# A float32 edge softmax: taking the maxima off in PSUM, in halves of 1024 columns, with part of the products on ScalarE

## The chip, the cores and the metric

One core of one Trainium2 chip. The metric is the device time of one launch in microseconds; less is better. The kernel is one program of four graph layers that run one after the other; the change touches the first of them only.

## The reference, cut to what matters

The first layer is an attention layer over E = 200,000 edges sorted by destination, with 16 x 16 = 256 logits per edge and a softmax of each of the 256 over the edges of one destination:

```
w_m = (efeat @ W_msg + b_msg).reshape(E, 16, -1)
w_a = (efeat @ W_attn + b_attn).reshape(E, 16, -1)
h_src = feat[src][:, :, None]
e1 = w_m * h_src
e2 = w_a * h_src
seg_max = segment_max(e2, dst)
ex = exp(e2 - seg_max[dst])
denom = segment_sum(ex, dst)
ft = segment_sum(e1 * (ex / denom[dst]), dst)
out = ft.sum(axis=1)
```

Its result goes through a layer normalisation into three more layers (a relational convolution, an edge-conditioned one and three convolutions with batch normalisation), which stay as they are. All is float32.

## The kernel before, in words

The edges are padded to 200,704 and cut into 128 chunks of T = 1568, one chunk to a partition. A block `b` takes TB0 = 8 neighbouring edges of every chunk (`q` = 0 to 7), so there are NB0 = 196 blocks; a tile `[128, 8, 256]` holds one block's 256 values per edge. The loop of blocks is written four at a time (U0 = 4), with four buffers of the loaded data, of the maxima M and of the sums ST, and two of e2, PX and cf.

Every engine has its own order of instructions, written out by hand, and they meet at semaphores only. `count(per, more)` in a wait is: so many per block in all blocks before, and `more` in this one.

- SP (`l0_sync`, L482) loads indices and turned edge features two blocks ahead, flags one block ahead, and stores the maxima and both kinds of sums, 1 MB each per block.
- POOL (`l0_pool`) gathers the eight source rows h of every partition, one indirect transfer for each q.
- TensorE (`weigh`, L543) multiplies the edge features of one q (17 rows, on one of four row groups of 32) with the attention or message weights, 256 float32 columns, into half a PSUM bank; one call does two q. Logits use banks 0 to 3, messages 4 to 7.
- VectorE (`l0_vector`) does the rest but the exponentials. For its block b: `logits` e2 = PSUM x h (L587), two q at a time; `forward` (L600) and `backward` (L608), the running maximum over the edges of one destination in both directions, a chain of 8 and one of 7 steps of 256 columns, each on the result of the last; `factor` (L620), the exponent cf that rescales the carried sums; and `less_maxima` (L614), e2 - M over all 2048 columns. For the block before, `last`: `exp_by_source` (L629), which multiplies the exponentials with h over 2048 columns; `carried` (L638); `messages` (L647), PSUM x that product, two q at a time; and `sum_step` (L654, L657), a chain of 8 running sums of 512 columns, numerator and denominator side by side.
- ScalarE (`l0_scalar`) takes Exp of cf (L571) and of all 2048 columns of e2 (L574).

The order of VectorE's instructions is that of `body` (L668). The steps of the three chains alternate there: between two steps of one chain stands an instruction of another.

Of the kernel before, what the change touches and what calls it, by code (L numbers as in the profile page):

```python
# [14 lines left out]
N, D = 6250, 16  # L15
# [105 lines left out]
def program(nc, io, out):  # L121
    ctx = ExitStack()
    with ctx:
# [337 lines left out]
        l_wa, l_wm, l_e2, l_fw, l_bw, l_a = sem("l_wa"), sem("l_wm"), sem("l_e2"), sem("l_fw"), sem("l_bw"), sem("l_a")  # L461
        l_ex, l_t, l_p, l_q, l_s = sem("l_ex"), sem("l_t"), sem("l_p"), sem("l_q"), sem("l_s")
# [4 lines left out]
        def l0_first_vector():  # L467
            V.memset(waug[:, :], 0.0).then_inc(*l_clear.up())
            V.memset(M[U0 - 1][:, TB0 - 1, :], 0.0).then_inc(*l_clear.up())
            V.memset(ST[U0 - 1][:, :, TB0 - 1, :], 0.0).then_inc(*l_clear.up())  # L470
            V.wait_ge(*l_clear.now())

# [9 lines left out]
        def l0_sync():  # L482
            def load_in(b):
                if due(n := b.on(-U0).count(4, 4)):
# [44 lines left out]
        def l0_pool():  # L529
            def gather(b):  # L530
                PO.wait_ge(l_in[b.k], b.slot(32, 32))
                if due(n := b.on(-U0).count(1, 1)):
                    PO.wait_ge(l_t, n)
                PO.nop(nofuse=True)
                for q in range(TB0):
                    PO.indirect_dma_start(h[b.k][:, q, :], None, io["x"],  # L536
# [5 lines left out]
        def l0_tensor():  # L542
            def weigh(b, n, message):  # L543
                if not message:
                    PE.wait_ge(l_in[b.k], b.slot(32, 32))
                if due(m := b.count(4, n - 1)):
                    PE.wait_ge(l_p if message else l_e2, m)
                for r in TWO:
                    row = 32 * (2 * (n % 2) + r)
                    mm = PE.matmul(PS[0:CH, 4 * message + 2 * (n % 2) + r, 0:C2], efT[b.k][row:row + D + 1, n // 2, :],  # L550
                                   waug[row:row + D + 1, C2 * message:C2 * message + C2])
                mm.then_inc(l_wm if message else l_wa, 1)

            def body(b):
                for n in range(4):
                    weigh(b, n, 0)
                if b.on(-1).exists():
                    for n in range(4):
                        weigh(b.on(-1), n, 1)

            def last(b):
                for n in range(4):
                    weigh(b, n, 1)
# [3 lines left out]
        def l0_scalar():  # L567
            def body(b):
                e, P = e2[b.k % 2], PX[b.k % 2]
                S.wait_ge(l_a, b.count(2, 2))  # L570
                S.activation(cf[b.k % 2][:, :], cf[b.k % 2][:, :], ACT.Exp).then_inc(l_ex, 1)  # L571
                if due(n := b.on(-2).count(TB0, TB0)):
                    S.wait_ge(l_s, n)
                S.activation(P[:, 0, :, :], e[:, :, :], ACT.Exp).then_inc(l_ex, 1)  # L574
# [3 lines left out]
        def l0_vector():  # L578
            def logits(b, n):
                ts = slice(2 * n, 2 * n + 2)  # L580
                if n == 0:
                    V.wait_ge(l_g[b.k], b.slot(16 * TB0, 16 * TB0))
                    if due(m := b.on(-2).count(2, 2)):
                        V.wait_ge(l_ex, m)
                V.wait_ge(l_wa, b.count(4, n + 1))
                bank = 2 * (n % 2)
                V.tensor_tensor(e2[b.k % 2][:, ts, :].rearrange("p t (i o) -> p t i o", i=D),  # L587
                                PS[0:CH, bank:bank + 2, 0:C2].rearrange("p t (i o) -> p t i o", i=D),
                                bc(h[b.k][:, ts, :], D, 3), ALU.mult).then_inc(l_e2, 1)

            def forward(b, q):
# [4 lines left out]
                V.wait_ge(l_e2, b.count(4, q // 2 + 1))  # L596
                if due(n := b.count(TB0, q)):
# [3 lines left out]
                                       in1=e2[b.k % 2][:, q, :], op0=ALU.add, op1=ALU.max).then_inc(l_fw, 1)  # L601
# [8 lines left out]

            def less_maxima(b):
                e = e2[b.k % 2]
                V.wait_ge(l_bw, b.count(TB0 - 1, TB0 - 1))
                V.tensor_tensor(e[:, :, :], e[:, :, :], M[b.k][:, :, :], ALU.subtract).then_inc(l_a, 1)  # L614
# [9 lines left out]
            def exp_by_source(b):  # L624
                P = PX[b.k % 2]
                V.wait_ge(l_ex, b.count(2, 2))
                if due(n := b.on(-2).count(TB0, TB0)):
                    V.wait_ge(l_s, n)
                V.tensor_tensor(P[:, 1, :, :].rearrange("p t (i o) -> p t i o", i=D),  # L629
                                P[:, 0, :, :].rearrange("p t (i o) -> p t i o", i=D),  # L630
                                bc(h[b.k][:, :, :], D, 3), ALU.mult).then_inc(l_t, 1)

            def carried(b):
                if due(n := b.slot(32, 0)):
                    V.wait_ge(l_st[b.k], n)
                if due(n := b.count(TB0, 0)):
# [4 lines left out]
            def messages(b, n):  # L641
                ts = slice(2 * n, 2 * n + 2)
                P = PX[b.k % 2]
                V.wait_ge(l_t, b.count(1, 1))
                V.wait_ge(l_wm, b.count(4, n + 1))
                bank = 4 + 2 * (n % 2)
                V.tensor_tensor(P[:, 1, ts, :], PS[0:CH, bank:bank + 2, 0:C2], P[:, 1, ts, :], ALU.mult).then_inc(l_p, 1)  # L647

            def sum_step(b, q):
                s, P = ST[b.k], PX[b.k % 2]  # L650
                V.wait_ge(l_p, b.count(4, q // 2 + 1))
                if q == 0:
                    V.wait_ge(l_q, b.count(1, 1))
                    V.tensor_tensor(s[:, :, 0, :], s[:, :, 0, :], P[:, :, 0, :], ALU.add).then_inc(l_s, 1)  # L654
                else:
                    V.wait_ge(l_s, b.count(TB0, q))
                    V.scalar_tensor_tensor(out=s[:, :, q, :], in0=s[:, :, q - 1, :], scalar=flb[b.k][:, q, 1:2],  # L657
                                           in1=P[:, :, q, :], op0=ALU.mult, op1=ALU.add).then_inc(l_s, 1)

            def sums_alone(b):  # L660
                exp_by_source(b)
                carried(b)
                for q in range(TB0):
                    if q % 2 == 0:
# [3 lines left out]
            def body(b):  # L668
                last = b.on(-1) if b.on(-1).exists() else None
                logits(b, 0)  # L670
                logits(b, 1)
# [1423 lines left out]
```

## Time and profile before

| | us |
|---|---|
| median of 3 runs | 14537.35 (14511.41 to 14591.29) |
| profiled execution | 14542.93 |
| its span, first to last instruction | 14541.7 |
| VectorE busy in the span | 11137.2 (77%) |
| TensorE busy | 8238.6 (57%) |
| ScalarE busy | 4787.7 (33%) |
| POOL busy | 8838.1 (61%) |

The first layer's blocks run from about 190 to 4480 us of the span. The page's second part cuts the span into 40 slices of 364 us; in the slices of the first layer VectorE shows 9 (90% or more), TensorE 2 and ScalarE 0 or 1, and the granted TensorE clock is 5 tenths of full speed; later layers show TensorE at 4 to 9 and the clock at 5 to 9 tenths. Busy time counts only how long instructions ran; how they follow one another is read from the timeline.

### The profile page before, as it was taken

How to read it: one execution, taken by the hardware profiler on the slowest of the kernel's cores; microseconds unless marked ns; L12 is line 12 of the kernel's file. 1: busy time of each engine (PE TensorE's matmuls, PEld its weight loads, DVE VectorE, ACT ScalarE, POOL GpSimd, SP SyncE). 2: the span in 40 equal slices, each digit the busy share in tenths (PEclk: the TensorE clock that was granted, in tenths of full speed). 3: DMA queues.
4: the chain of work that ended last, by engine and by line, in shares of the span. 5: the costliest groups of instructions: out<-in, count | busy, mean ns of one | idle time of the engine just before them, and what ended most of it. 6: DMA issues, size and time to landing. Idle time of an engine off the chain costs nothing. (4 is left out here: it accounts for less than half of the span.)

```text
span 14541.7 us, 147837 instructions
## 1 busy us (share of the span) xinstructions
PE 8238.6 (57%) x41291; PEld 5764.4 (40%) x41291; DVE 11137.2 (77%) x19230; ACT 4787.7 (33%) x2765; POOL 8838.1 (61%) x6976
## 2 busy tenths in 40 slices
PE   1222222222220489689746565665678858985886
PEld 0111111111110367567523233332456646664664
DVE  6999999999998768578645455554578868886886
ACT  0110110110110368467501110110057746774774
POOL 5555555555553377678745555555168857885886
PEclk5555555555555799899867787777789979997997
DMA  2444444444442222222211111111033323332332
GB/s 81 157 150 155 157 152 153 157 154 151 157 155 94 68 68 84 60 71 82 55 45 37 38 36 37 36 35 38 16 102 111 112 74 105 112 106 80 111 110 70
DMA packets 629773, 1371.10 MB, mean 94 GB/s; under 512 B 262833, under 2 KB 403118, under 8 KB 554126
## 3 DMA queue, kind: packets, MB, share of 16 engines
q1 hardware_dynamic: 405534, 1076.25, 20.2%
q0 software_dynamic: 224112, 293.30, 8.8%
q8 instruction: 62, 1.02, 0.0%
q14 instruction: 65, 0.53, 0.0%
HBM read 656.16 MB, written 712.80 MB: 94 GB/s over the span
## 5 line engine op out<-in xcount | busy, mean ns | idle before, releaser
L536 POOL DMA_INDIRECT h<-in_x,idx x1568 | 2252.1, 1436 | 2000.3 <-DMA efT<-in_edge_attr_t 1561.3
L550 PE MATMUL PS<-waug,efT 17*128 17x256 f32 x6272 | 1129.7, 679 | 3165.9 <-DVE e L587 2178.7
L1684 PE MATMUL PS<-hot,lhs 128*128 128x392 bf16 x9408 | 1829.2, 352 | 1221.8 <-issue 644.4
L1671 POOL DMA_INDIRECT myg<-node_table,mix x1568 | 1644.5, 1049 | 1310.0 <-DVE mmsg L1740 782.1
L550 PEld LDWEIGHTS PS<-waug,efT 17*128 17x128 f32 x6272 | 696.7, 314 | 3598.4 <-DVE e L587 2225.4
L1684 PEld LDWEIGHTS PS<-hot,lhs 128*128 128x128 bf16 x9408 | 949.9, 102 | 2101.4 <-issue 1028.9
L1305 PE MATMUL PS<-every_weight,dstf 112*128 112x144 f32 (+1 forms) x8960 | 1346.4, 296 | 533.2 <-DVE dstf L1405 376.1
L1305 PEld LDWEIGHTS PS<-every_weight,dstf 112*128 112x128 f32 x8960 | 1268.1, 200 | 717.6 <-DVE dstf L1405 197.1
L1755 DVE TENSOR_TENSOR lhs<-mkx,m 128x512 bf16<-128x512 bf16 x1176 | 428.9, 419 | 1402.8 <-remote 1065.4
L571 ACT ACTIVATE cf<-cf 128x256 f32<-128x256 f32 x196 | 81.7, 417 | 3842.8 <-DVE e L614 3842.8
L1283 POOL DMA_INDIRECT c0yg<-node_table,c0ix x672 | 935.8, 1393 | 533.1 <-DMA c0ix<-in_src 287.4
L1283 POOL DMA_INDIRECT c2yg<-node_table,c2ix x672 | 952.9, 1418 | 276.6 <-issue 204.5
L1283 POOL DMA_INDIRECT c1yg<-node_table,c1ix x672 | 944.9, 1406 | 289.5 <-issue 204.2
L657 DVE SCALAR_TENSOR_TENSOR ST<-ST,flb,PX 128x512 f32<-128x512 f32 x1372 | 1016.3, 741 | 0.7
L1283 POOL DMA_INDIRECT r1yr<-node_table,r1ix x672 | 832.0, 1238 | 283.0 <-issue 204.2
L1283 POOL DMA_INDIRECT r0yr<-node_table,r0ix x672 | 828.4, 1233 | 271.0 <-issue 204.2
L1335 ACT ACTIVATE r0hot<-r0hb 128x3584 fp32r<-128x3584 bf16 x224 | 717.0, 3201 | 535.5 <-DVE r0hb L1391 329.9
L1295 PE MATMUL PS<-c2hot,parts 128*112 128x512 f32 x3136 | 842.7, 416 | 34.7 <-ACT c2hot L1335 29.2
L1295 PE MATMUL PS<-c0hot,parts 128*112 128x512 f32 x3136 | 840.8, 415 | 32.3 <-ACT c0hot L1335 27.1
L1295 PE MATMUL PS<-c1hot,parts 128*112 128x512 f32 x3136 | 834.7, 413 | 33.4 <-ACT c1hot L1335 27.6
L1335 ACT ACTIVATE r1hot<-r1hb 128x3584 fp32r<-128x3584 bf16 x224 | 716.9, 3201 | 396.4 <-DVE r1hb L1391 196.8
L1295 PE MATMUL PS<-r1hot,parts 128*112 128x512 f32 x3136 | 811.6, 410 | 25.4 <-ACT r1hot L1335 25.0
(393 smaller groups left out, 18688.7 us busy)
## 6 DMA issues: line engine op xcount, KB each, us to landing
softmax_maxima<-M SPq DMA_DIRECT2D x196, 1024.0 KB, 8.2
softmax_denominators<-ST SPq DMA_DIRECT2D x196, 1024.0 KB
softmax_numerators<-ST SPq DMA_DIRECT2D x196, 1024.0 KB
r0rb<-pick_b SPq DMA_DIRECT2D x56, 512.0 KB
r0ra<-pick_a SPq DMA_DIRECT2D x56, 512.0 KB
r1rb<-pick_b SPq DMA_DIRECT2D x56, 512.0 KB
r1ra<-pick_a SPq DMA_DIRECT2D x56, 512.0 KB
c0rb<-pick_b SPq DMA_DIRECT2D x56, 512.0 KB
```

What stands on the lines that cost most here:

```text
L536: PO.indirect_dma_start(h[b.k][:, q, :], None, io["x"], bass.IndirectOffsetOnAxis(ap=idx[b.k][:, q:q + 1], axis=0))\
L550: mm = PE.matmul(PS[0:CH, 4 * message + 2 * (n % 2) + r, 0:C2], efT[b.k][row:row + D + 1, n // 2, :], waug[row:row + D + 1, C2 * message:C ...
L571: S.activation(cf[b.k % 2][:, :], cf[b.k % 2][:, :], ACT.Exp).then_inc(l_ex, 1)
L657: V.scalar_tensor_tensor(out=s[:, :, q, :], in0=s[:, :, q - 1, :], scalar=flb[b.k][:, q, 1:2], in1=P[:, :, q, :], op0=ALU.mult, op1=ALU.ad ...
L1283: PO.indirect_dma_start(to, None, table, bass.IndirectOffsetOnAxis(ap=ix[b.k][:, q:q + 1], axis=0))\
L1295: mm = PE.matmul(PS[0:A9 * D, 4 + q % 2, :], parts[:, m % 2, m // 2, :], hot_[q % 2][:, m // 2, :], start=(m == 0), stop=(m == 2 * KT - 1))
L1305: mm = PE.matmul(weighed(q)[:, r, 0:R * D], mx[q % 2][:, 128 * r:128 * r + 128], every[0:A9 * D, 0:R, :].rearrange("p r o -> p (r o)"))
L1335: S.activation(hot_[q % 2][:, :, :], hb[q // 2 % 2][:, :, at:at + 512], ACT.Copy).then_inc(h_cv.sem, 1)
L1671: PO.indirect_dma_start(yg[b.k][:, q, :], None, table8, bass.IndirectOffsetOnAxis(ap=ix[b.k][:, q:q + 1], axis=0))\
L1684: mm = PE.matmul(PS[:, 6 + k, 0:A7 // 2], lhs[(G * b.k + q) % 2][:, r, part, :], hot[4 * ((G * b.k + q) % 2) + r][:, k * A7 // 2:(k + 1) * ...
L1755: V.tensor_tensor(lhs[(G * b.k + q) % 2][:, :, n, :].rearrange("p t (a f) -> p t a f", a=8), mkx[b.k][:, 4 * q:4 * q + 4, :, :], bc(m3[b.k ...
```

## The change

- The eight q of a block are laid out by `at(q) = 2 * (q % 4) + q // 4`: bank n holds q = n and q = n + 4. A bank is now full (512 columns), all four logit banks `wa` belong to one block until its exponentials are taken, and likewise the four message banks `wm`.
- Weights, logits and messages work on halves: half 1 is banks 2 and 3 (q 2, 6, 3, 7), half 0 banks 0 and 1. A half is four matmuls of 256 columns and one VectorE instruction of 1024 columns. The logits' weights of half 1 wait for the Exp of half 1 of the block before, those of half 0 for its Exp of half 0.
- `less_maxima` leaves VectorE. TensorE first copies the logits e2 back into their bank by a matmul with the identity (`put_back`, 128 rows, 512 float32 columns, an open accumulation), and when the backward steps that a bank needs are done it adds minus identity times M (`less_maxima`). The order is bank 3, 2, 1, 0; bank 3 needs four backward steps, bank 0 all seven.
- ScalarE takes Exp straight from PSUM, half 1 first, then Exp of cf, then makes the product with h for tiles 6 and 7 (q 3 and 7) by 32 ACTIVATE instructions of 16 columns each, with h as the per-partition scale. `exp_by_source` keeps the other six tiles (1536 columns). The messages of half 1 wait for ScalarE's products.
- The order of VectorE is new; backward 0 to 6 stand together, and so do sum steps 4 to 7.

```diff
+        minus = sb("minus_ident", [128, 128], F32, L)
+        wa = PS[0:CH, 0:4, :].rearrange("p b (t c) -> p (b t) c", c=C2)
+        wm = PS[0:CH, 4:8, :].rearrange("p b (t c) -> p (b t) c", c=C2)
+        def at(q):
+            return 2 * (q % 4) + q // 4
         def l0_first_vector():
+            V.tensor_scalar(minus[:, :], ident[:, :], -1.0, None, ALU.mult).then_inc(*vd.up())
...
         def l0_tensor():
+            def weigh(b, half, message):
+                if message:
+                    if due(m := b.on(-1).count(2, half + 1)):
+                        PE.wait_ge(l_p, m)
+                else:
                     PE.wait_ge(l_in[b.k], b.slot(32, 32))
+                    if due(m := b.on(-1).count(3, 2 - half)):
+                        PE.wait_ge(l_ex, m)
+                for q in (2 * half, 2 * half + 1, 2 * half + 4, 2 * half + 5):
+                    row = 32 * (q % 4)
+                    mm = PE.matmul((wm if message else wa)[:, at(q), :], efT[b.k][row:row + D + 1, q // 4, :],
                                    waug[row:row + D + 1, C2 * message:C2 * message + C2])
                 mm.then_inc(l_wm if message else l_wa, 1)
+            def put_back(b, n):
+                PE.wait_ge(l_e2, b.count(2, 2 - n // 2))
+                PE.matmul(PS[0:CH, n, :], ident[:, :], e2[b.k % 2][:, 2 * n:2 * n + 2, :], start=True, stop=False)
+            def less_maxima(b, n):
+                PE.wait_ge(l_bw, b.count(TB0 - 1, TB0 - 1 - n))
+                mm = PE.matmul(PS[0:CH, n, :], minus[:, :], M[b.k][:, n::4, :], start=False, stop=True)
+                if n % 2 == 0:
+                    mm.then_inc(l_le, 1)
             def body(b):
+                for half in (1, 0):
+                    weigh(b, half, 0)
                 if b.on(-1).exists():
+                    for half in TWO:
+                        weigh(b.on(-1), half, 1)
+                for n in (3, 2, 1, 0):
+                    put_back(b, n)
+                for n in (3, 2, 1, 0):
+                    less_maxima(b, n)
...
         def l0_scalar():
+            def exp_half(b, half):
+                S.wait_ge(l_le, b.count(2, 2 - half))
                 if due(n := b.on(-2).count(TB0, TB0)):
                     S.wait_ge(l_s, n)
+                S.activation(PX[b.k % 2][:, 0, 4 * half:4 * half + 4, :], wa[:, 4 * half:4 * half + 4, :], ACT.Exp).then_inc(l_ex, 1)
+            def body(b):
+                exp_half(b, 1)
+                exp_half(b, 0)
+                S.wait_ge(l_a, b.count(1, 1))
+                S.activation(cf[b.k % 2][:, :], cf[b.k % 2][:, :], ACT.Exp).then_inc(l_ex, 1)
+                S.wait_ge(l_ex, b.count(3, 2))
+                for t in (6, 7):
+                    for i in range(D):
+                        act = S.activation(PX[b.k % 2][:, 1, t, D * i:D * i + D], PX[b.k % 2][:, 0, t, D * i:D * i + D], ACT.Copy,
+                                           scale=h[b.k][:, t, i:i + 1])
+                act.then_inc(l_x, 1)
...
-                V.tensor_tensor(e[:, :, :], e[:, :, :], M[b.k][:, :, :], ALU.subtract).then_inc(l_a, 1)
...
+                V.tensor_tensor(P[:, 1, 0:6, :].rearrange("p t (i o) -> p t i o", i=D),
+                                P[:, 0, 0:6, :].rearrange("p t (i o) -> p t i o", i=D),
+                                bc(h[b.k][:, 0:6, :], D, 3), ALU.mult).then_inc(l_t, 1)
```

VectorE's `body` after the change, in order (calls with `last` are left out in the first block):

```
logits(b, 1)   logits(b, 0)   forward(b, 0)   exp_by_source(last)   forward(b, 1)   carried(last)
forward(b, 2)  messages(last, 0)  forward(b, 3)  forward(b, 4)  sum_step(last, 0)  forward(b, 5)
forward(b, 6)  sum_step(last, 1)  forward(b, 7)  messages(last, 1)  backward(b, 0) ... backward(b, 6)
sum_step(last, 2)  sum_step(last, 3)  factor(b)  sum_step(last, 4) ... sum_step(last, 7)
```

POOL's gather waits also for `l_x` of four blocks ago, and the input load for both message halves of four blocks ago.

## Rows read from the trace of the kernel before

**Rows 1.** Windows: stretch, length, busy time of each engine, clock, DMA share, GB/s.
```profile
200.00:4400.00 4200.00, 1107.74 (x6163) 684.57 (x6165) 4132.09 (x6744) 427.59 (x386) 2231.40 (x1551) 0.50 0.42 153
```
**Rows 2.** Groups by form, 400 to 4200 us: count, busy, mean ns, idle before.
```profile
L647 DVE TENSOR_TENSOR PX<-PS,PX 128x512 f32<-128x512 f32 x698 | 474.4, 680 | 0.0
...
L614 DVE TENSOR_TENSOR e<-e,M 128x2048 f32<-128x2048 f32 x175 | 398.9, 2279 | 0.0
L574 ACT ACTIVATE PX<-e 128x2048 f32<-128x2048 f32 x174 | 329.5, 1894 | 0.0
```
**Rows 3.** Waits, 400 to 4200 us: who waited for whom, total, times, longest.
```profile
ACT cf L571 <- DVE e L614: 3404.6, 174, 19.6
...
DVE e L587 <- PE PS L550: 58.2, 174, 0.3
```
**Rows 4.** Timeline, VectorE, one block: start, duration, instruction.
```profile
1999.47 2.27 DVE L614 TENSOR_TENSOR e<-e,M 128x2048 f32<-128x2048 f32 x1
...
2019.79 0.48 DVE L608 SCALAR_TENSOR_TENSOR M<-M,flb 128x256 f32<-128x256 f32 x1
2020.19 0.74 DVE L657 SCALAR_TENSOR_TENSOR ST<-ST,flb,PX 128x512 f32<-128x512 f32 x1
2020.85 0.47 DVE L620 SCALAR_TENSOR_TENSOR cf<-M,flb 128x256 f32<-128x256 f32 x1
...
2021.25 2.28 DVE L614 TENSOR_TENSOR e<-e,M 128x2048 f32<-128x2048 f32 x1
2023.45 0.74 DVE L657 SCALAR_TENSOR_TENSOR ST<-ST,flb,PX 128x512 f32<-128x512 f32 x1
```
**Rows 5.** Timeline, VectorE, the first block.
```profile
205.32 3.48 DVE L600 SCALAR_TENSOR_TENSOR M<-M,flb,e 128x256 f32<-128x256 f32 x6
...
208.84 4.04 DVE L608 SCALAR_TENSOR_TENSOR M<-M,flb 128x256 f32<-128x256 f32 x7
```
**Rows 6.** Timeline, the last block's sums.
```profile
4469.43 1.22 PE L550 MATMUL PS<-waug,efT 17*128 17x256 f32 x4 [9.27 <-DVE PX L647]
...
4471.59 1.60 DVE L657 SCALAR_TENSOR_TENSOR ST<-ST,flb,PX 128x512 f32<-128x512 f32 x2
...
4473.11 0.68 DVE L647 TENSOR_TENSOR PX<-PS,PX 128x512 f32<-128x512 f32 x1
4473.83 1.60 DVE L657 SCALAR_TENSOR_TENSOR ST<-ST,flb,PX 128x512 f32<-128x512 f32 x2
```
**Rows 7.** Timeline, TensorE in a later layer: one record, eight, eight.
```profile
5039.84 0.58 PE L1305 MATMUL PS<-every_weight,dstf 112*128 112x128 f32 x1 [3.65 <-DVE dstf L1405]
...
5039.84 2.07 PE L1305 MATMUL PS<-every_weight,dstf 112*128 112x128 f32 x8 [3.65 <-DVE dstf L1405]
...
5046.65 1.06 PE L1305 MATMUL PS<-every_weight,dstf 112*128 112x128 f32 x8
```
**Rows 8.** Timeline and windows of two bursts after pauses, columns as in Rows 1.
```profile
10954.20 2.28 PE L1305 MATMUL PS<-every_weight,dstf 112*128 112x144 f32 x8 [4.44 <-DVE dstf L1405]
...
10954.20:10957.20 3.00, 3.00 (x11) 2.75 (x12) 3.00 (x7) 3.00 (x2) 2.70 (x2) 0.50 0.55 200
10957.20:10957.45 0.25, 0.25 (x2) 0.20 (x1) 0.25 (x2) 0.25 (x1) 0.25 (x1) 0.77 0.00 0
...
14296.00 2.29 PE L1305 MATMUL PS<-every_weight,dstf 112*128 112x144 f32 x8 [4.22 <-DVE dstf L1405]
...
14296.00:14302.00 6.00, 6.00 (x18) 4.89 (x19) 5.41 (x11) 6.00 (x4) 5.08 (x4) 0.50 0.39 126
14302.00:14302.50 0.50, 0.50 (x3) 0.38 (x2) 0.50 (x2) 0.50 (x1) 0.50 (x1) 0.62 0.90 361
```
**Rows 9.** ScalarE: a group by form, and two rows of the timeline.
```profile
L2008 ACT ACTIVATE mean<-mean 128x16 f32<-128x16 f32 x2 | 0.4, 216 | 193.2 <-DVE mean L1987 193.2
...
4487.62 0.31 ACT L762 ACTIVATE w<-w 128x128 f32<-128x128 f32 x1 [21.77 <-DVE w L795]
...
4487.84 0.29 ACT L763 ACTIVATE w<-w 128x128 f32<-128x128 f32 x1
```

More of the change, by code:

```diff
@@ L471, in l0_first_vector @@
             V.wait_ge(*l_clear.now())
+            V.wait_ge(*vd.now())
         def l0_first_sync():
@@ L561, in last @@
             def last(b):
-                for n in range(4):
-                    weigh(b, n, 1)
+                for half in TWO:
+                    weigh(b, half, 1)
             loop(PE, body, NB0, TB0, last=last, u=U0)
         def l0_scalar():
[L568 to L571, printed above, removed]
+            def exp_half(b, half):
+                S.wait_ge(l_le, b.count(2, 2 - half))
@@ L576, in l0_scalar, with logits @@
             loop(S, body, NB0, TB0, u=U0)
         def l0_vector():
-            def logits(b, n):
-                ts = slice(2 * n, 2 * n + 2)
-                if n == 0:
+            def logits(b, half):
+                ts = slice(4 * half, 4 * half + 4)
+                if half == 1:
                     V.wait_ge(l_g[b.k], b.slot(16 * TB0, 16 * TB0))
[L583 to L586, printed above, removed]
+                V.wait_ge(l_wa, b.count(2, 2 - half))
@@ L587, in logits @@
                 V.tensor_tensor(e2[b.k % 2][:, ts, :].rearrange("p t (i o) -> p t i o", i=D),
-                                PS[0:CH, bank:bank + 2, 0:C2].rearrange("p t (i o) -> p t i o", i=D),
+                                wa[:, ts, :].rearrange("p t (i o) -> p t i o", i=D),
                                 bc(h[b.k][:, ts, :], D, 3), ALU.mult).then_inc(l_e2, 1)
@@ L669, in body @@
                 last = b.on(-1) if b.on(-1).exists() else None
+                logits(b, 1)
                 logits(b, 0)
-                logits(b, 1)
                 forward(b, 0)
-                logits(b, 2)
+                if last:
+                    exp_by_source(last)
                 forward(b, 1)
-                logits(b, 3)
+                if last:
+                    carried(last)
                 forward(b, 2)
                 if last:
-                    exp_by_source(last)
+                    messages(last, 0)
                 forward(b, 3)
-                if last:
-                    carried(last)
                 forward(b, 4)
                 if last:
-                    messages(last, 0)
+                    sum_step(last, 0)
                 forward(b, 5)
+                forward(b, 6)
+                if last:
+                    sum_step(last, 1)
+                forward(b, 7)
                 if last:
                     messages(last, 1)
-                forward(b, 6)
-                if last:
-                    sum_step(last, 0)
-                forward(b, 7)
-                if last:
-                    sum_step(last, 1)
-                backward(b, 0)
+                for n in range(7):
+                    backward(b, n)
                 if last:
                     sum_step(last, 2)
-                backward(b, 1)
-                if last:
-                    messages(last, 2)
-                backward(b, 2)
-                if last:
-                    sum_step(last, 3)
-                backward(b, 3)
-                if last:
-                    sum_step(last, 4)
-                backward(b, 4)
-                if last:
-                    messages(last, 3)
-                backward(b, 5)
-                if last:
-                    sum_step(last, 5)
-                backward(b, 6)
-                if last:
-                    sum_step(last, 6)
+                    sum_step(last, 3)
                 factor(b)
-                less_maxima(b)
-                if last:
-                    sum_step(last, 7)
+                for q in range(4, TB0):
+                    if last:
+                        sum_step(last, q)
             loop(V, body, NB0, TB0, last=sums_alone, u=U0)
```

52 lines of the change are left out of this document (20 added, 32 removed).

## The prediction, made before the changed kernel was run

> **What bounds the kernel now.** The windows come first: in the stretch of the first layer VectorE is busy 4132 of 4200 us, TensorE 1108 at a granted clock of 0.50, ScalarE 428 [rows 1]. The groups of that stretch and the waits say the same: ScalarE's idle time is a wait for the subtraction L614, and VectorE itself waits only for the logits' weights, 0.33 us a block (58.2 us over 174) [rows 2, 3]. So a block lasts as long as VectorE's instructions follow one another. The timeline gives their spacing: L614 begins at 1999.47 and again at 2021.25, so a block is 21.78 us, and there are 196. There also an instruction that does not need the one in front starts 0.08 us before that one's end: a step follows a 256-column one after 0.40 (duration 0.48), a sum step after 0.66 (0.74), L614 after 2.20 (2.28) [rows 4].
>
> **What leaves VectorE's block.** L614 goes: 2.20. L629 falls from 2048 to 1536 columns; between 512 columns (0.680) and 2048 (2.279) a column costs 1.04 ns, so 0.53 [rows 2]. Four logit and four message instructions of 512 columns become two and two of 1024: 4 x 0.60 against 2 x (0.680 + 0.534 - 0.08) = 2.27, so 0.13 for each kind, 0.26. The 0.33 wait was for a matmul that started only after the first logits; the new weights of a half are asked for before them, and I take it as gone (what is late in its place comes below). Sum: 3.32.
>
> **What the new order adds.** Before, between two steps of one chain stood an instruction of another chain. The new order puts dependent steps back to back: forward 3-4 and 5-6, all of backward 0 to 6, sum steps 2-3 and 4-5-6-7. Counting the pairs: 2 + 6 + 4 = 12, and forward 0 right behind the second logits. The first block, which has no sums of a predecessor, shows what such a pair costs: six forward steps take 3.52 us from 205.32 to 208.84, 0.587 each, not 0.40; so +0.19 [rows 5]. In the last block two sum steps take 1.60 together, so they start 0.86 apart, not 0.66: +0.20; and a sum step starts 0.72 behind the message instruction that it needs, not 0.60: +0.12 [rows 6]. Sum: 8 x 0.19 + 4 x 0.20 + 0.12 = 2.44. VectorE's own block becomes 21.78 - 3.32 + 2.44 = 20.90, 0.88 less.
>
> The Trainium skill, "VectorE: DVE Perf Modes", section "The DRAIN you can't avoid", speaks against that addition: instructions with and without a semaphore between them took the same time. By it the 2.44 is nothing and VectorE's block 18.46 us. This trace does not agree for this chain (0.587 against 0.40 for one line of one kernel); the rival that follows from it is below.
>
> **The new path through TensorE and ScalarE.** The maxima are now taken off in PSUM. Let t = 0 be when the matmul for bank 3 may begin, just behind the fourth backward step. VectorE then has two steps at 0.587, one at 0.40, sum 2 0.86, sum 3 0.66, factor 0.40, sums 4 to 6 at 0.86 and sum 7 0.66: the next block's first logits (half 1) could start at 6.78 and the second (half 0) at 7.91. Before them lie, in this order: four matmuls of `minus` by 512 float32 columns; weights of half 1 (their banks are free after the first Exp, which fits beside the last two matmuls); Exp of half 0; weights of half 0; logits.
> - A matmul: eight records of 128 float32 columns take 2.07 us at the low clock (1.2 GHz) and 1.06 at the high one (2.4 GHz) [rows 7]. There are two records to a float32 matmul; one alone lasts 0.58, so they follow at (2.07 - 0.58) / 7 = 0.213 us per 128 columns; 512 columns in two records are 1.70 us low and 0.85 high. Four: 6.82 or 3.41.
> - Exp of 1024 columns: between 16 columns (0.216, [rows 9]) and 2048 (1.894, [rows 2]) a column is 0.826 ns: 1.05.
> - Weights of a half: two matmuls on two row groups took 1.22 at the low clock [rows 6], 0.85 of it columns. The half has four on two row groups, so 2.07 low, and about 1.1 high (bounds 0.7, if all four ran side by side, and 2.07).
> - So the second logits may start at e + 0.30 (drain) + 0.06 + 1.05 + 0.06 + 1.1 + 0.05 = e + 2.6, where e is when the four matmuls have streamed. They are late when e > 5.3. The first logits (e + 1.15 against 6.78) are never the tighter ones.
>
> e hangs on the clock. It is 0.50 through the whole stage now [rows 1]. After a pause of over 4 us a dense burst starts at the low clock and gets the high one later: in 38 such bursts of this trace after 3.1 to 6.4 us, mean 4.5; the shortest and the longest are shown (0.50 for 3.00 us, then 0.77 in the next 0.25; 0.50 for 6.00, then 0.62 in the next 0.50) [rows 8]. The new TensorE stream has that form. Behind the four matmuls come the weights and the four copies of e2 back into PSUM, done near t = 13, and the next four matmuls start at 20.9: a pause of about 8 us, and each burst starts low. If the clock rises at r, e = 3.41 + r/2, late for r > 3.78; over the 38 values of r the mean lateness is 0.5 us a block. It lies on VectorE's path, since nothing is queued there ahead of the logits. The ends for this wait are 0 and 2.50 (all low: 6.82 + 0.30 + 0.06 + 1.05 + 0.06 + 2.07 + 0.05 = 10.41 against 7.91). I take 0.5.
>
> **ScalarE's 32 products.** They begin near t = 7.4 (e 5.67, both Exps, `cf` 0.41) and must be done for the messages of half 1, 9.5 us behind the second logits, at 17.9: 10.5 us for 32, or 0.33 each. The nearest rows: a 16-column ACTIVATE lasts 0.216, and a 128-column one follows its predecessor by 0.22 [rows 9]; so 4.4 (0.216 less an overlap of 0.08) to 7.0 us. Hidden, price 0; without the cover each 0.1 us more per product than 0.33 would be 3.2 us a block. The Trainium skill, "ScalarE: Activation LUTs", section "What ACT_TABLE_LOAD costs", adds a fixed piece of about 93 ns for a per-partition scale, and an overlap of the same size; an estimate by it is 32 x 0.20 = 6.4 us, hidden too; no row before has such a scale.
>
> **Nothing.** The four copies back start at t = 9 and even at the low clock end before 17, ahead of 20.9. Input loads wait on SP for the message weights and gathers on POOL additionally for ScalarE's products of four blocks ago; both are prefetched two blocks and long met. The maxima are stored earlier, the sums as before. DMA is at 0.42 [rows 1] and would be at 0.43. `minus` is one instruction of under 0.3 us.
>
> **Sum.** -0.88 + 0.5 = -0.38 us a block, x 196 = -74 us. The profiled execution took 14543 (span 14541.7); so 14469, and the median of the runs, 14537, lies 6 below the profiled one. I say 14468, with 14410 to 14525 for this case (lateness 0.2 to 0.8).
>
> **Rivals.**
> - *TensorE is never late* (the clock stays high over the pause, or rises at once): -0.88 a block, -172 us, 14370. For it: pauses of 4.1 to 4.3 us sometimes left the clock high. Against: none of more than 5 us did, and this one is 8. Chance 0.13.
> - *The matmuls run at the low clock and TensorE sets the block* (slower). Place: between the fourth backward step and the second logits. All low: -0.88 + 2.50 = +1.62, +318 us, 14861. It decides from a mean lateness of 0.88, that is from e = 6.2 or from weights that need 0.4 us more than my 1.1. For it: the stage is at 0.50 now and my margin is thin. Against: float32 bursts later in this trace do get the high clock [rows 8]. Chance 0.24, most of it between +0 and +150.
> - *ScalarE's products are late*: above 0.33 us each; at 0.40 the block is 2.2 us longer and the time 14900. Chance 0.05.
> - *Back-to-back chains cost nothing*: block 18.46; but then the 6.78 and 7.91 shrink by 1.4, lateness is about 1.6, and the block 20.1: -1.7, -335 us, 14208. Only a change of behaviour between first block and loop would bring it. Chance 0.03. The section on the drain named above is its ground.
> - My forecast: 0.55.
>
> **How the numbers follow.** About 0.5% (73 us) is what a measurement can tell here. The forecast lies on that bound, so half of its 0.55 is faster by more and half is not. Faster: 0.26 of it, with the first rival's 0.13 and the fourth's 0.03, is 0.42. Same: 0.27 of it and 0.05 of the second rival, 0.32. Slower: the second rival's other 0.19, ScalarE's 0.05, and 0.02 of my own case: 0.26. The range runs from 14360 (first rival) to 14650 (the second up to a lateness of 1.45); outside are the drain rival, ScalarE's and the upper third of the second, under 0.2.
>
> **What would show it.** In the profile after: no L614 group on VectorE, L629's at about 1.75 us; backward steps 0.58 to 0.59 apart; float32 matmuls of 128x512 at two durations, the subtraction mostly in the slow one and the copies back in the fast one; granted clock of the stage between 0.55 and 0.8; the only VectorE wait in the stage before the half-0 logits, on TensorE, 0.2 to 0.8 us a block; ScalarE idle before its next Exp. Wrong if the clock stays 0.50, if VectorE waits for the products, or if the wait is above 0.9 us.

## The result: slower, by a stall that no step of the prediction had

The changed kernel took 14751.52 us (median of 4 runs, 14720.96 to 14781.33) against 14534.86 (14511.41 to 14591.29) for the kernel before on the same chip: ratio 1.0143, 95% interval 1.0107 to 1.0180, so 1.4% slower. I had said 14468, faster, 14360 to 14650. The profiled execution took 14740.64, its span 14739.4.

The windows of the first layer after the change, columns as in [rows 1], do not look like a slower kernel: VectorE is less busy than before, TensorE more, at a higher clock.

```profile
200.00:4400.00 4200.00, 2467.52 (x8742) 1154.34 (x8743) 3577.29 (x5452) 1581.45 (x6361) 1572.93 (x1465) 0.74 0.40 145
```

VectorE's busy time fell from 4132 to 3577 us of 4200, and it is still the engine that sets the stage. The rest is idle time, and the waits (400 to 4200 us, columns as in [rows 3]) name it:

```profile
DVE e L625 <- issue: 331.1, 58, 8.3
DVE e L625 <- PE PS L567: 61.3, 66, 1.4
DVE M L638 <- DVE e L625: 34.3, 165, 0.2
DVE ST L692 <- DVE ST L692: 19.5, 41, 0.5
```

"issue" is a wait for nothing that the profile shows. The timeline of VectorE (start, duration, instruction, idle time before it) shows it in front of the first logits of every fourth block; rows in between are left out:

```profile
1907.09 2.41 DVE L625 TENSOR_TENSOR e<-PS,h 128x1024 f32<-128x1024 f32 x2
...
1927.87 2.52 DVE L625 TENSOR_TENSOR e<-PS,h 128x1024 f32<-128x1024 f32 x2 [0.20 <-PE PS L567]
...
1939.81 3.61 DVE L646 SCALAR_TENSOR_TENSOR M<-M,flb 128x256 f32<-128x256 f32 x7
1943.34 1.60 DVE L692 SCALAR_TENSOR_TENSOR ST<-ST,flb,PX 128x512 f32<-128x512 f32 x2
...
1945.26 3.31 DVE L692 SCALAR_TENSOR_TENSOR ST<-ST,flb,PX 128x512 f32<-128x512 f32 x4
1956.47 2.36 DVE L625 TENSOR_TENSOR e<-PS,h 128x1024 f32<-128x1024 f32 x2 [7.90 <-issue]
1959.05 0.48 DVE L638 SCALAR_TENSOR_TENSOR M<-M,flb,e 128x256 f32<-128x256 f32 x1 [0.22 <-DVE e L625]
...
1978.13 2.41 DVE L625 TENSOR_TENSOR e<-PS,h 128x1024 f32<-128x1024 f32 x2 [1.39 <-PE PS L567]
...
1996.63 2.48 DVE L692 SCALAR_TENSOR_TENSOR ST<-ST,flb,PX 128x512 f32<-128x512 f32 x3 [0.47 <-DVE ST L692]
1999.23 2.41 DVE L625 TENSOR_TENSOR e<-PS,h 128x1024 f32<-128x1024 f32 x2
```

The blocks take 20.8, 28.6, 21.7 and 21.1 us, and so on: 92.1 for four. Four blocks are one pass of the loop, so the 7.9 us (8.3 at the most) lie at its back edge, the jump from its last instruction to its first, and 1.4 more follow one block later. The mean of 40 passes is 92.16. TensorE explains neither the place nor the length. It works at its own weights in the first 2.1 us of the gap, then waits for VectorE; only afterwards is it slow and late:

```profile
1941.92 5.53 PE L577 MATMUL PS<-M,minus_ident 128*128 128x512 f32 x8 [8.30 <-DVE M L646]
1947.37 3.30 PE L567 MATMUL PS<-waug,efT 17*128 17x256 f32 x32
1957.75 6.14 PE L573 MATMUL PS<-e,ident 128*128 128x512 f32 x8 [7.08 <-DVE e L625]
1970.37 6.66 PE L577 MATMUL PS<-M,minus_ident 128*128 128x512 f32 x8 [6.48 <-DVE M L646]
```

The page's third part has another trace of it (queue, kind: packets, MB, share). One of the two lines of instruction queues was `q14 instruction: 65, 0.53, 0.0%` before and is now:

```profile
q14 instruction: 299, 2.44, 0.0%
```

The other line, `q8 instruction`, hardly moved (62 and 64 packets). A packet of q14 is 8 KB (2.44 MB over 299). Asked for in short windows, the new packets come five to a pass; in the pass above they start at 1945.41, 1948.91, 1954.74, 1958.63 and 1997.32, two of them inside the gap (1948.57 to 1956.47) and the last 0.7 us behind the end of the 0.47 wait. The reading that the experiments put to the test: VectorE's instructions are fetched anew in each pass, and it waits for them.

From the first logits to the first copy out of PSUM behind the layer the stage was 4284.1 us and is 4525.1: +241.0. The whole profiled execution is only 197.7 longer; the later layers, which the change does not touch, took about 44 less, and I have no cause for that.

### The profile page after: what moved, and what is told of

It reads as the page before. It is cut to its first block and busy times, and to the rows that moved or that the text cites. A ratio compares the mean times of both kernels' runs of the same rounds, so it can differ in the third digit from the quotient of the medians.

```text
span 14739.4 us, 160571 instructions
## 1 busy us (share of the span) xinstructions
PE 9775.6 (66%) x44427; PEld 6319.8 (43%) x44427; DVE 10793.1 (73%) x18251; ACT 6059.7 (41%) x9233; POOL 8359.8 (57%) x6976
## 3 DMA queue, kind: packets, MB, share of 16 engines
q14 instruction: 299, 2.44, 0.0%
## 5 line engine op out<-in xcount | busy, mean ns | idle before, releaser
L549 POOL DMA_INDIRECT h<-in_x,idx x1568 | 1683.1, 1073 | 2810.4 <-DMA efT<-in_edge_attr_t 1858.4
L1689 POOL DMA_INDIRECT myg<-node_table,mix x1568 | 1682.3, 1073 | 1275.3 <-DVE mmsg L1758 750.0
L577 PE MATMUL PS<-M,minus_ident 128*128 128x512 f32 x1568 | 1167.1, 913 | 1495.3 <-DVE M L646 1488.6
L603 ACT ACTIVATE PX<-PS 128x1024 f32<-128x1024 f32 x392 | 401.3, 1024 | 2809.8 <-PE PS L577 2251.8
L577 PEld LDWEIGHTS PS<-M,minus_ident 128*128 128x128 f32 x1568 | 452.8, 304 | 2201.2 <-DVE M L646 1749.5
L613 ACT ACTIVATE PX<-PX,h 128x16 f32<-128x16 f32 x6272 | 1264.3, 295 | 8.8 <-issue 8.8
L573 PE MATMUL PS<-e,ident 128*128 128x512 f32 x1568 | 866.4, 703 | 353.2 <-DVE e L625 342.3
```

The source lines that it names most:

```text
L549: PO.indirect_dma_start(h[b.k][:, at(q), :], None, io["x"], bass.IndirectOffsetOnAxis(ap=idx[b.k][:, q:q + 1], axis=0))\
L573: PE.matmul(PS[0:CH, n, :], ident[:, :], e2[b.k % 2][:, 2 * n:2 * n + 2, :], start=True, stop=False)
L577: mm = PE.matmul(PS[0:CH, n, :], minus[:, :], M[b.k][:, n::4, :], start=False, stop=True)
L613: act = S.activation(PX[b.k % 2][:, 1, t, D * i:D * i + D], PX[b.k % 2][:, 0, t, D * i:D * i + D], ACT.Copy, scale=h[b.k][:, t, i:i + 1])
L1689: PO.indirect_dma_start(yg[b.k][:, q, :], None, table8, bass.IndirectOffsetOnAxis(ap=ix[b.k][:, q:q + 1], axis=0))\
```

## The experiments

A *filler* is a number of one-column memsets on VectorE ahead of the first layer's loop (0.06 us each, and 240 in a row take 7.1). They move the code; the first logits wait for their data meanwhile and start within 1 us of where they did:

```
         V.wait_ge(*vd.now())
+        filler = sb("filler", [128, N], F32, L)
+        for k in range(N):
+            V.memset(filler[:, k:k + 1], 0.0)
```

The places 209 to 429 and the like in the first expectations leave out the separate wait and register instructions. In the compiled stream the loop of the changed kernel is 269 instructions, 318 to 586, and that of the kernel before 303, 339 to 641; the table uses these. "Stage" is measured as above; it was 4284.1 us for the kernel before. The runs fall into four groups on different chips; the median of the kernel before, run beside each, was 13686 (e1 to e4), 13661 (one run, e5 to e8), 13700 (e9 to e12) and 14493 us (e13 to e15). The first layer takes the same on all of them (4284.1, 4283.8 and 4284.2 for two-page forms of the kernel before; 4525.1 and 4525.9 for the changed one), so whole times are compared only within a group, stages everywhere. After, e1, e9, e12, e13 and e15 are medians of 4 or 5 runs, the others are single runs, and the effects read from them are read from the stage.

| run | loop at (start mod 256) | pages touched | q14 packets | stage | whole |
|---|---|---|---|---|---|
| after, as given | 318 (62) | 3 | 299 | 4525.1 | 14751.52 |
| e13, the same again | 318 (62) | 3 | 298 | 4525.9 | 14716.28 |
| e5, filler 256 | 574 (62) | 3 | 300 | 4508.4 | 13924.48 |
| e14, filler 249 | 567 (55) | 3 | 300 | 4369.9 | 14575.66 |
| e9, filler 4 | 322 (66) | 2 | 68 | 4036.6 | 13454.85 |
| e1, filler 32 | 350 (94) | 2 | 69 | 4034.8 | 13443.15 |
| e2, filler 64 | 382 (126) | 2 | 70 | 4036.3 | 13457.96 |
| e10, filler 240 | 558 (46) | 2 | 70 | 4036.6 | 13445.77 |
| e3, before, filler 32 | 370 (114) | 2 | 66 | 4283.8 | 13701.49 |
| e6, before, filler 239 | 577 (65) | 2 | 67 | 4284.2 | 13678.14 |
| e11, before, filler 215 | 553 (41) | 3 | 296 | 4290.4 | 13719.44 |

"Pages" are taken here as runs of 256 instructions whose boundaries lie at 64 modulo 256. The rows of the table leave 63 to 65; the idle times pick 64, since one falls in front of place 320 in the changed kernel and one between 575 and 578 in e14. What the rows do not fix is the length: runs of 128 with a boundary at 64 modulo 128 fit them as well, with four touched where the table says 3 and three where it says 2. The traces speak for the 128: each packet is 8 KB, the stream has just passed 448 and 576 at two of the five packets of a pass of the changed kernel, and the 0.47 wait is in front of place 448, in the middle of a page of 256. A loop of this length that starts at 180 to 191 modulo 256 would decide it; no run has one. "Page" and "three pages" below can be read either way.

**e1, filler 32.**


> The changed kernel with 32 one-column memsets of a spare tile on VectorE ahead of the first layer's loop, nothing else: its loop of 220 instructions then stands at instructions 241 to 461 of VectorE's program and not at 209 to 429. Theory (fetch of VectorE's loop): in the changed kernel VectorE idles 7.9 us at each back edge of the first layer's loop, where the loop before, at 226 to 472, idled nothing; the loop now lies across a boundary of the instruction memory, and every jump back waits for a fetch. With the shift the 7.9 us go; 47 iterations, so some 370 to 400 us less than the changed kernel, near 14350 to 14400, faster than before by about 1%. Rival (ScalarE's 32 small instructions a block, or TensorE's longer loop, are what is fetched and waited for): nothing changes, 14750.

Blocks of 20.48 us, no stall: 0.9821 of the kernel before (0.9805 to 0.9837). The stage is 490 us shorter and not 370 to 400, since the waits that follow the stall go with it. The lost time is the stall, and the place of the code decides on it.

**e2, filler 64, and e3, the kernel before with filler 32.**


> The same with 64 memsets: the loop stands at 273 to 493. Theory: boundaries are 256 instructions apart; both kernels' behaviour puts one 30 to 39 instructions short of a count of 256 and the next at 473 to 482, so this loop crosses the second one and the 7.9 us at each jump are back: within 40 us of the changed kernel's 14750. Rival (the filler helps because it delays the start or separates the engines): like the run with 32.

> The kernel before with the same 32 memsets: its loop of 246 instructions moves from 226-472 to 258-504. Theory: it then crosses the second boundary and gets a stall of about 8 us at each of its 47 jumps, +350 to +400 us, 14900, with nothing of the change in it. Rival (the stall comes from the new work on ScalarE and TensorE): 14537, no change.

Both missed: no stall, 20.48 and 21.78 us a block. The distance of the loop's ends to a boundary, as I counted it then, is not the rule.

**e4, products on VectorE.** ScalarE's `for t in (6, 7)` products and their waits go, VectorE's product has `0:8` for `0:6`; the loop starts at the same place and has 268 instructions.


> The changed kernel with ScalarE's 32 products a block left to VectorE again (one instruction of 2048 columns for all eight tiles), and the waits for them gone; ScalarE's loop falls from 163 to 31 instructions, VectorE's stays at 209 to 429. Theory: the 7.9 us at each jump stay; each block costs 0.53 us more on VectorE, 104 us in all, if none of it is hidden: 14800 to 14860. Rival (ScalarE's instruction stream causes the stall): it goes, 14750 - 380 + 104 = 14470.

The stall stayed (7.9 to 8.3 us, 295 packets, stage 4562.8), with ScalarE's loop some 130 instructions shorter. So it is not ScalarE's stream; that it is VectorE's, e1 had shown, whose fillers stand in VectorE's stream alone.

**e5, filler 256, and e6, the kernel before with filler 239.**


> 256 one-column fills ahead of VectorE's loop of the first layer instead of 32: the loop lies at its instructions 465 to 685, that is 256 further than in the changed kernel (209 to 429), which stalled 7.9 us at each back edge; with 32 fills (241 to 461) and 64 (273 to 493) there was no stall. Theory A (the place within 256-instruction pages decides; the Trainium skill, Runtime: NRT & Kernel Launch, section Instruction fetch mechanics, states such pages): the stall is back, blocks of 20.8 to 21.1 us and one of 29 in every four, the stage about 4525 us, the instruction queue near 300 packets. Theory B (another period, or the absolute place): no stall, blocks of 20.48, the stage near 4036 us, some 70 packets.

> The kernel before with 239 one-column fills: its VectorE loop lies at 465 to 711 instead of 226 to 472. Nothing of the change is in it. Theory A (a loop that begins some instructions ahead of a page of 256 and reaches far into the next one loses its first page, whatever it computes): a stall of about 8 us each four blocks, the stage 4284 + 46 x 8.5 = 4675 us, the whole about 390 us above the kernel before. Theory B (the stall needs the new order or the new path through TensorE): the stage stays at 4284 us and the time at that of the kernel before plus some 20 us for the fills.

e5 brings the stall back, as a period of 256 (or of 128) wants. e6 missed: no stall, stage 4284.2. That sent me to the compiled stream, and to pages *touched* by the loop.

**e9, filler 4, and e10, filler 240**: on either side of the twelve starts (52 to 63) from which 269 instructions touch three pages.


> Only 4 one-column fills ahead of VectorE's loop. Counted with the separate wait instructions, the compiled loop of the changed kernel is 269 instructions long (318 to 586; the counts in the expectations so far left the waits out), that of the kernel before 303 (339 to 641). The places so far agree with pages of 256 instructions of which two are held, with a boundary at 64 modulo 256: the changed kernel (start 62) and the one with 256 fills (start 574, which is 62) touch three pages, the first with two instructions; the kernel before with 239 fills (start 577, which is 65) touches two and did not stall. Theory A (three pages): with 4 fills the start is 66, two pages, no stall: blocks of 20.48, stage near 4036 us, time near 0.982 of the kernel before. Theory B (the end near a boundary, within the first third of a page, makes the stall): the end moves only from 74 to 78, the stall stays, stage 4508 to 4525 us.

> 240 fills: the loop lies at 558 to 826, modulo 256 from 46 to 58. Theory A (a third page is needed only if the loop starts at 52 to 63): two pages, no stall, stage near 4036 us. Theory B (the loop starts ahead of a boundary and ends in the first third of a page behind another): the stall is there, stage 4508 to 4525 us.

Theory A held in both: no stall, stages of 4036.6. Four instructions worth nothing are worth 489 us of stage (4525.9 in e13 against 4036.6). e9's waits, 400 to 4000 us, in full:

```profile
DVE M L641 <- DVE e L628: 36.6, 176, 0.2
DVE e L628 <- PE PS L570: 3.1, 20, 0.2
```

and its row of the instruction queue:

```profile
q14 instruction: 68, 0.56, 0.0%
```

**e11, the kernel before with filler 215.**


> The kernel before with 215 fills: its loop of 303 instructions lies at 553 to 855, modulo 256 from 41. Its pages are three (boundary at 64: 23 instructions, 256, 24). Theory A: it stalls now, about 8 us each four blocks (46 back edges, 370 us): stage near 4650 us where the same kernel with 239 fills had 4284, time near 14050. Rival (only the changed kernel's code stalls): 4284 us, 13680.

Half right. The kernel before makes the fetches now, 296 packets for the 67 of e6, with its code as it was:

```profile
q14 instruction: 296, 2.42, 0.1%
```

But it loses 0.12 to 0.2 us a pass and not 8. VectorE's sequencer, which takes instructions from the stream and runs some way ahead of the engine, shows where a part of the rest is. Its rows (`DVEq`) of the loop's line have the jump back and the first instruction behind it; duration in ns, then the start. e11, and e9 for comparison:

```profile
L100 DVEq COMPARE_BRANCH  x1: 63/63/63, 2023.9 to 2023.9; - x1
L100 DVEq FUSED_REGOPS  x1: 63/63/63, 2026.7 to 2026.7; - x1
```
```profile
L100 DVEq COMPARE_BRANCH  x1: 56/56/56, 2084.3 to 2084.3; - x1
L100 DVEq FUSED_REGOPS  x1: 63/63/63, 2084.6 to 2084.6; - x1
```

The step over the jump takes 0.3 us with two pages and, with three, 2.8 in e11, 2.9 in the changed kernel and 3.0 in e14. So e11 has this stall too and hides it: when its sequencer jumps at 2023.9, VectorE still has the subtraction (2024.02, 2.27 us) and a sum step in hand, until 2026.96, and the next logits start at 2026.99. The changed kernel has only one sum step in hand there, until 0.7 us behind the jump. The second half of the 7.9 is missing in e11: the next packet comes 2.4 us after the one at the jump, in the changed kernel and in e14 5.8 us after it. e11's first page holds 23 instructions (at 87.1 us for 303 some 6.6 us of work) and its third 24, where the changed kernel has 2 and 11. That this split makes the difference is argued and not shown.

**e13, the changed kernel again.**


> The changed kernel itself, unchanged, beside the others of this call: its loop touches three pages. Expected: a stall of 7.9 us each four blocks, stage 4508 to 4525 us, and some 480 us more than with 4 fills (13455 when it ran), so 13930, a ratio to the kernel before of 1.015 to 1.02. If it ran near 13460 here, the stall would hang on something else than the place of the code.

1.0152 (1.0114 to 1.0190), the stall as before.

**e14, filler 249**: the same loop, 9 instructions in the first page and 4 in the third.


> 249 fills: VectorE's loop lies at 567 to 835, modulo 256 from 55: 9 instructions in the first page (two of registers, both logits, forward 0 and their waits), 256, and 4 in a third. Theory: three pages make two fetches one after the other at each back edge, and what stalls is the second, which comes 7.9 us after VectorE has run dry in the changed kernel; the instructions in the first page cover a part of it. Both logits and forward 0 take 2.8 us, so the idle time is 5.1 us, in front of the source-row product and no longer of the logits. Stage 4036 + 47 x (5.1 + 0 to 1.4 follow-up) = 4280 to 4345 us. Rival (the stall is one length whatever lies in the first page): 7.9 us, 4508 or more. Rival (it belongs to logits alone): none.

VectorE's waits, 400 to 4000 us, and the two of one pass:

```profile
DVE PX L665 <- issue: 106.3, 40, 2.9
DVE e L628 <- issue: 103.4, 41, 2.8
DVE e L628 <- PE PS L570: 50.2, 88, 1.2
```
```profile
1984.09 2.36 DVE L628 TENSOR_TENSOR e<-PS,h 128x1024 f32<-128x1024 f32 x2 [2.52 <-issue]
...
1989.66 1.76 DVE L665 TENSOR_TENSOR PX<-PX,h 128x1536 f32<-128x1536 f32 x1 [2.51 <-issue]
```

The sum, 5.0, is the 5.1 I had worked out (7.9 less 2.8 of work in the first page), but it comes in two pieces: 2.5 at the back edge, and 2.5 where the second page begins (place 576 in this stream, the source-row product). In both kernels the stream goes on behind that boundary 8.5 to 8.6 us after the jump. In the changed kernel nothing of VectorE's data work lies in the first page, its boundary is in front of the logits, and one gap of 7.9 is all that is seen. The stage is above my 4280 to 4345: a pass takes 88.75 us, 6.8 more than in e9, of which the two pieces are 5.2 on average and the waits for TensorE 1.2. The rest is not accounted for.

**e7, subtraction on VectorE, and e8, products on VectorE**, both with filler 32. e7 puts `tensor_tensor(e, e, M, subtract)` back behind the factor, drops `put_back` and `less_maxima` from TensorE and lets Exp read `e2`; e8 is e4's edit.


> The changed kernel with 32 fills (no stall) and the maxima taken off by VectorE again, one instruction of 2048 columns behind the factor; no float32 matmuls with identity or its negative, Exp reads SBUF. If the PSUM path is worth what my sum gave it (2.20 a block and nothing late): 20.48 + 2.20 = 22.7 us a block, the stage 4036 + 431 = 4467 us. Rival: the matmuls cost VectorE time that the order hid, then the block is shorter than 22.5.

> The changed kernel with 32 fills (no stall) and all source-row products on VectorE: its instruction has 2048 columns for 1536, ScalarE has no products. By my sum 0.53 us a block more: 21.0 us, the stage 4036 + 104 = 4140 us. Rival: the 32 instructions of ScalarE slow VectorE (they share SBUF) or delay it; then the block is shorter than 20.9.

Per block, from the stages 4446.1, 4201.5 and e1's 4034.8 over 196: the subtraction in PSUM is worth 2.10 us (my term: 2.20), the products on ScalarE 0.85 (0.53). Of the latter 0.3 is a wait of VectorE for TensorE's weights that came up in e8 (53.8 us over 86 in 400 to 4000). So e7 came near its 4467, and e8 missed its 4140. Each rests on one run. In e7, without the float32 matmuls of 512 columns, the granted clock of the stage is back at 0.50 (0.83 in e9).

**e12 and e15, other orders of VectorE's work**, both with filler 4. (l logits, f forward, b backward, s sum, m messages, x source product, c carried, F factor.)

```
after: l1 l0 f0 x f1 c f2 m0 f3 f4 s0 f5 f6 s1 f7 m1 b0..b6 s2 s3 F s4..s7
e12:   l1 l0 x f0 c f1 m0 f2 s0 f3 m1 f4 s1 f5 f6 f7 b0..b4 s2 b5 s3 b6 s4 F s5..s7
e15:   l1 l0 x f0 c f1 m0 f2 s0 f3 m1 f4 f5 f6 f7 b0..b4 s1 b5 s2 b6 s3 F s4..s7
```


> 4 fills and another order of the same VectorE instructions: source-row product directly behind the second logits, messages of half 1 between forward 3 and 4, sum 1 between forward 4 and 5, sums 2, 3 and 4 between backward 4, 5, 6 and the factor. One dependent pair of maxima steps (0.12) and two of sum steps (0.20) less, and no wait of 0.20 for forward 0: 0.7 us a block, 19.8, stage 3900 us, 135 us below filler 4 alone. Between the fourth backward step and the second logits VectorE has 7.3 us of work, and TensorE and ScalarE needed about 7.4. Rival: TensorE's path is now the later one; VectorE waits 0.5 us or more before the half-0 logits, and the block stays at 20.3 or above.

> The interleaved order had VectorE waiting 0.69 us a block for the half-1 weights: from the first matmul of the burst to the first logits 6.67 us, and VectorE's work in that stretch is 6.0. Here sum 1 also moves behind backward 4 (sums 1, 2, 3 between backward 4, 5, 6 and the factor, sums 4 to 7 behind it): one sum step of 0.66 more in the stretch, 6.8 in all, so nothing is late. Against filler 4: three dependent pairs of sums for four (0.20) and no wait at forward 0 (0.20): 0.4 us a block, 20.08, stage 3955 us, 80 us less than 13455: 13375. Rival: the chain through TensorE and ScalarE is itself 20.48 long around the block whatever VectorE's order, then 4036 again.

e12 gained nothing over e9 (13451.45 and 13454.85): VectorE's order is 0.7 us a block shorter and it waits 0.7 for TensorE. The waits of e12 in 400 to 4000 us, and of e15:

```profile
DVE e L628 <- PE PS L570: 125.5, 176, 0.8
```
```profile
DVE e L628 <- PE PS L570: 50.0, 156, 0.5
DVE e L628 <- issue: 12.9, 50, 0.4
```

e15 missed too: blocks of 20.28 to 20.73 us where 20.08 was due, stage 4045.9, 0.9822 of the kernel before (0.9790 to 0.9854). The groups of the subtraction on TensorE in e9 and in e15 show what gave way, the mean time of one:

```profile
L580 PE MATMUL PS<-M,minus_ident 128*128 128x512 f32 x1408 | 955.4, 838 | 1442.3 <-DVE M L649 1442.3
```
```profile
L580 PE MATMUL PS<-M,minus_ident 128*128 128x512 f32 x1408 | 1048.7, 914 | 1348.7 <-DVE M L649 1348.7
```

A longer stretch behind the fourth backward step was eaten by a slower burst (914 ns for 838; 862 in e12); the granted clock of the stage fell from 0.83 to 0.80.

Two limits that happen to meet do not explain this. From the sixth pass on a pass takes 81.92 us on average, four times 20.48, in e1, e2, e9, e10, e12 and e15 alike, in three orders of VectorE's work (each pass within 0.03 us of it, in e15 within 0.25); in e9 it comes down to that from 84.24, in e1 up from 81.80. The windows of one block of e9 and one of e12, cut where the granted clock changes, columns as in [rows 1]:

```profile
2013.59:2020.41 6.82, 3.50 (x4) 1.50 (x5) 6.57 (x13) 0.00 (x0) 4.99 (x6) 0.50 0.05 5
2020.42:2034.07 13.65, 8.72 (x45) 4.30 (x43) 13.11 (x19) 8.69 (x35) 3.54 (x3) 1.00 0.65 244
```
```profile
2009.97:2016.79 6.82, 3.78 (x5) 1.72 (x6) 6.51 (x14) 0.00 (x0) 5.30 (x6) 0.50 0.05 5
2016.80:2030.44 13.64, 8.58 (x44) 4.20 (x43) 12.74 (x18) 8.69 (x35) 4.21 (x4) 1.00 0.65 244
```

The clock goes low and high once in each block, and rises 3.5 us behind the start of the burst of subtractions in e9 (2016.91), 3.8 us behind it in e12 (2013.01) and 4.1 to 4.9 in e15. A block that tries to be shorter has its burst start earlier against the rise, with more of its matmuls at the low clock, and so the time comes back as a wait for TensorE. That the block is held in step with the clock in this way is what the figures suggest; no run holds the clock and changes the order, so it is not shown.

## Why the prediction was wrong

**The step that failed is "Sum": -0.38 us a block, times 196.** It took all blocks as alike, and the paragraph "Nothing" had no entry for the way VectorE gets its instructions. Shorter by 34 instructions, the loop also began 21 earlier in the stream, at 62 for 83 modulo 256, and so touched three pages for two. Each pass of four blocks then costs 7.90 at the back edge, 0.47 in front of place 448, 1.39 for TensorE's lateness behind the stall, and 0.20 in front of one more pair of logits: 9.96 of the 92.08 - 4 x 20.48 = 10.16 that a pass takes more than four blocks of e9. Over 47 passes that is 478 us; e13 less e9 measures 489. With it, my own 14468 would have been near 14950, so the rest of the sum erred by some 200 us the other way: 21.40 us a block where e9 has 20.48, 180 us, and the later layers. That the measured time lies where the slower rival had its numbers (up to 14861) is luck: its place and its cause were others.

The Trainium skill, "Runtime: NRT & Kernel Launch", section "Instruction fetch mechanics", states blocks of 256 instructions, two of them held, sequential prefetch, and a fetch before execution goes on when a taken branch leaves the window. I did not weigh it. The runs agree with the stall at a taken branch (2.8 to 3.0 us for 0.3 at the jump) and with two blocks held, if a block is 256 instructions; by the 8 KB packets and the wait at place 448 what is fetched at a time may be 128. They show the price that the page does not give (7.9, 5.0 or 0.1 us a pass), and add that the loop of the kernel before is above 256 instructions as well and costs nothing so long as it touches two.

**The other steps, read from e9 where the stall is gone:**
- *What leaves the block, 3.32*: held as far as runs show it. e7 gives 2.10 for the subtraction (2.20), and the source-row product took 1.75 as said; the other 0.59 has no run of its own.
- *What the order adds, 2.44*: too much. Seven backward steps take 3.61, so (3.61 - 0.48) / 6 = 0.52 each in the loop and not the 0.587 of the first block [rows 5]: 8 x 0.07 = 0.5 less. Sum pairs held (1.60 for two, 0.85 apart). Forward 0 starts 0.21 behind the end of the second logits, 0.29 later than an independent instruction and not 0.12. My 20.90 becomes 20.54; measured 20.48.
- *Lateness, 0.5*: nothing (3.1 us in 3600). The matmuls of the subtraction lasted 0.84 us a record, the copies back 0.61, so the burst did start slow. The size that was wrong is r: I took 38 values of other bursts, mean 4.5, with lateness above 3.78, and in e9 it was 3.48 to 3.53 in every block from 20 to 180. With 3.5 my path gives 7.8 us from the start of the burst to the second logits; they start at 7.7 (its 0.30, 0.06 and 0.05 stand on no row). Where VectorE does wait for TensorE, 0.7 in e12 and 1.4 in the changed kernel, it is in front of the first logits, which I had called never the tighter ones.
- *ScalarE's products*: hidden. All 32 took 6.44 us, 0.20 each, the estimate of 6.4; a single one lasts 0.295, longer than my nearest row:

```profile
L613 ACT ACTIVATE PX<-PX,h 128x16 f32<-128x16 f32 x5280 | 1063.2, 295 | 0.0
```
- *The rivals*: the slower one named TensorE at the low clock; the place was wrong, and the stage's clock rose from 0.50 to 0.74. "TensorE is never late" (14370) is what e9 shows once the stall is gone: -1.30 us a block with the cheaper pairs, a ratio of 0.9824 (0.9807 to 0.9840).
- *Slips in the sums*: the terms given for 6.78 add to 6.73, the 14468 leaves out the 6 us that the same sentence takes off (14463), and the drain rival's 1.4 is 1.2. None matters beside 480.

## What to carry to other kernels

Before an edit that changes the number of instructions ahead of or in a hot loop, count the engine's compiled stream, waits and register instructions included: a loop of more than 256 can touch three pages, and then each back edge may cost microseconds whatever the edit saves. How much is seen depends also on the work that the engine has in hand at the jump: 3 us of it hid a stall of 2.8 in e11. The signs are an idle time put down to "issue" at one place per pass and a packet count of the instruction queue that grows with the passes; a few empty instructions ahead of the loop tell it apart from all else in one run. And when shorter orders all come back to the same block time, look at where the granted clock rises within the block before looking for a second limit (e12, e15).

## What was not expected of the hardware

- Four memsets of one column (322 for 318) took 489 us out of a stage of 4526.
- Instruction fetches are not a cost in themselves: e11 makes as many as the changed kernel (296 packets), its sequencer stands for 2.8 us at each jump, and it loses 6 us over the stage.
- The stall has two parts, and work in the first page covers some of the second one: 2.5 + 2.5 with 9 instructions there, 7.9 in one piece with 2. Which instructions each packet carried the traces do not say.
- Six kernels with three orders of VectorE's work settle at the same 81.92 us a pass, with the clock's rise at a fixed place in the block (3.5 us into the burst in e9).
- The same dependent step is spaced 0.587 us in the blocks ahead of the loop and again in the four behind it, and 0.52 in the loop. In the compiled stream the wait for the step before is an instruction of its own in the straight code and part of the step itself in the loop; no run tells whether that is the cause.
